# Spacing the first scores evenly over a turn, and putting the sums of exponentials last in ScalarE's slots

## The reference

```python
scores = einsum('bsnh,btnh->bnst', k, q) / sqrt(32)
scores = triu(scores) + -10000.0 * tril(ones, k=-1)
attn = softmax(scores, axis=2)
out = einsum('bnkq,bknh->bqnh', attn, v)
```

## Time and profile before

| what | us |
|---|---|
| median of 3 runs | 2469.89 (2462.67 to 2474.62) |
| the profiled execution, its own time | 2468.07 |
| its span in the trace | 2466.2 |
| TensorE busy | 2206.6 (89%) |
| ScalarE busy | 1648.3 (67%) |
| VectorE busy | 1519.0 (62%) |
| turns 2 to 15 | 1675.4, about 119.7 each |
| turn 16 | 113.0 |
| the experts | 425 |

### The profile page before, as it was taken

How to read it: one execution, slowest core, us unless ns; L and a number is a source line. 1 busy time by engine, 2 the same in 40 slices (tenths; PEclk the granted TensorE clock), 3 DMA queues, 4 the chain that set the end, 5 groups by cost and what they waited for, 6 DMA issues and landing times. The chain is left out here.

```text
span 2466.2 us, 48192 instructions
## 1 busy us (share of the span) xinstructions
PE 2206.6 (89%) x13674; PEld 1127.8 (46%) x13674; DVE 1519.0 (62%) x4937; ACT 1648.3 (67%) x4025; POOL 1125.4 (46%) x1622
## 2 busy tenths in 40 slices
PE   6679999999999999899989999999997776999997
PEld 3334444444444444344444444444443334666664
DVE  4545666666666575657666666666656554666664
ACT  5778686867676777677767767676765414666664
POOL 3223244444444443434444444444343534777775
PEclk9789999999999999999999999999998997999999
DMA  6022222222222222222222212121212017888885
GB/s 225 14 58 67 62 72 67 66 62 61 61 61 62 61 61 61 62 61 61 61 62 61 78 44 79 44 78 44 78 30 75 27 39 219 233 233 235 234 235 114
DMA packets 180907, 222.51 MB, mean 90 GB/s; under 512 B 37824, under 2 KB 119840, under 8 KB 180672
## 3 DMA queue, kind: packets, MB, share of 16 engines
q1 hardware_dynamic: 154048, 177.58, 24.4%
q0 software_dynamic: 26624, 42.12, 7.7%
HBM read 112.65 MB, written 56.46 MB: 69 GB/s over the span
## 5 line engine op out<-in xcount | busy, mean ns | idle before, releaser
L741 ACT ACTIVATE junk<-junk,nmax 128x512 f32<-128x512 f32 (+3 forms) x1024 | 571.6, 566 | 147.1 <-DVE nmax L1044 141.8
L1044 DVE CUSTOM_DVE_ANT_0 junk<-scores,maskrow 128x512 f32<-128x512 f32 (+3 forms) x1024 | 467.4, 487 | 192.9 <-PE scores L587 152.2
L731 ACT ACTIVATE probs<-scores_T 128x512 f32<-128x512 f32 x640 | 379.4, 600 | 69.1 <-PE scores_T L604 68.0
L1207 POOL TENSOR_SCALAR_AFFINE_SELECT probs<-probs 128x256 f32<-128x256 f32 x512 | 194.1, 415 | 383.4 <-ACT probs L731 383.0
L587 PE MATMUL scores<-stack_k,stack_q 96*128 96x512 f16 (+3 forms) x1024 | 252.0, 308 | 90.7 <-DVE nmax L1044 87.5
L1216 POOL DMA_INDIRECT slots_dram<-rec,idx x256 | 262.5, 1025 | 119.5 <-issue 106.9
L604 PE MATMUL scores_T<-stack_q,stack_k 97*128 97x512 f16 (+3 forms) x1024 | 252.8, 309 | 51.2 <-ACT probs L731 31.1
L1193 POOL TENSOR_TENSOR xres<-xres,bo 128x512 f32<-128x512 f32 x64 | 81.2, 1271 | 280.8 <-DMA xres<-in_x 280.8
L741 ACT ACTIVATION_READ_ACCUMULATOR junk<-junk,nmax 128x1 f32 x1024 | 207.3, 202 | 0.0
L211 PE MATMUL dense<-xT_hi,wqkv_hi 128*128 128x512 f16 x512 | 198.2, 387 | 1.5 <-DVE xT_lo L1014 1.5
L587 PEld LDWEIGHTS scores<-stack_k,stack_q 96*128 96x128 f16 x1024 | 97.1, 100 | 223.4 <-DVE nmax L1044 132.2
(11 more groups left out here) (234 smaller groups left out, 5560.3 us busy)
## 6 DMA issues: line engine op xcount, KB each, us to landing
stack_q<-split_q SPq DMA_DIRECT2D x384, 64.0 KB, 2.0
stack_k<-split_k SPq DMA_DIRECT2D x384, 64.0 KB, 2.4
out<-xres SPq DMA_DIRECT2D x67, 256.0 KB, 3.0
x2n<-in_x SPq DMA_DIRECT2D x64, 256.0 KB, 3.4
xres<-in_x SPq DMA_DIRECT2D x64, 256.0 KB, 2.7
x2n_dram<-x2n SPq DMA_DIRECT2D x16, 1024.0 KB, 4.4
ex_raw_wg<-in_W_gate SPq DMA_DIRECT2D x32, 512.0 KB
ex_raw_wu<-in_W_up SPq DMA_DIRECT2D x32, 512.0 KB
```

Source lines behind the costliest of these rows:

```text
L731: act.activation(to, at, ACT.Exp, scale=SCALE / (QS * QS)).then_inc(exp_done, 1)
L741: last = act.activation(x, x, ACT.Exp, scale=-1.0, bias=c["nmax"][:, hg % 2, m:m + 1], accum_out=c["sums"][:, hg % 2, m:m + 1])
L1044: last = dve.tensor_tensor_reduce(out=c["junk"][:, JUNK_AT[f], at:at + cols], in0=ps["scores"][f % 2][:, at:at + cols], in1=c["maskrow"][: ...
L1207: last = pool.affine_select(out=blk, in_=blk, compare_op=ALU.is_ge, fill=0.0, base=0, pattern=[[0, 2], [1, P]], channel_multiplier=-1)
```

## The change

Two edits. The first sets the slots of the first scores: one fill every two or three slots for group 1, and every three slots for groups 2, 3 and 0 over the rest of the turn. Since `MAX_SLOT`, `SUM_SLOT`, `NM_SLOT`, `SHIFT_SLOT` and `INV_SLOT` are derived from them, the maxima, the sums, the placing of the maxima and the inverses move along. The second edit moves `sums` and `shift_exps` behind everything else that ScalarE does in the same slot.

```diff
-S_AT = {1: range(1, 21, 2), 2: (23, 25, *range(31, 47, 2)), 3: (47, 49, 51, 53, *range(61, 73, 2)),
-        0: (83, 91, 94, 96, 99, 101, 104, 107, 110, 113)}
+S_AT = {1: (1, 4, 6, 9, 11, 14, 16, 19, 21, 24), 2: (27, 29, 32, 35, 38, 41, 44, 47, 50, 53),
+        3: (56, 59, 62, 65, 68, 71, 74, 77, 80, 83), 0: (86, 89, 92, 95, 98, 101, 104, 107, 110, 113)}
...
                     if attn and slot in READ_SLOT:
                         den_copy(i - 1, READ_SLOT[slot])
-                    if slot in SUM_SLOT:
-                        q, f = SUM_SLOT[slot]
-                        of = score_group(i, q, proj, attn)
-                        if of:
-                            sums(*of, f)
-                    if slot in SHIFT_SLOT:
-                        of = score_group(i, SHIFT_SLOT[slot], proj, attn)
-                        if of:
-                            shift_exps(*of)
                     if in_first(i) and slot in SPLIT_SLOT:
...
                     if attn and slot in AHI_SLOT:
                         att_hi(i - 1, AHI_SLOT[slot])
+                    if slot in SUM_SLOT:
+                        q, f = SUM_SLOT[slot]
+                        of = score_group(i, q, proj, attn)
+                        if of:
+                            sums(*of, f)
+                    if slot in SHIFT_SLOT:
+                        of = score_group(i, SHIFT_SLOT[slot], proj, attn)
+                        if of:
+                            shift_exps(*of)
```

## The result

| | before | after |
|---|---|---|
| median, us | 2468.66 (4 runs, 2462.67 to 2474.62) | 2557.03 (4 runs, 2554.61 to 2567.89) |
| ratio after to before | | 1.0372 [1.034, 1.0404] |
| span of the profiled execution | 2466.2 | 2552.6 |

The account below looks back on a forecast made before the run. TensorE, busy 2206.6 us, sets the pace. Terms 1.8 + 2.7 - 0.4 - 4.4 + 2.8 + 0.5 - 0.3 give 2.7 us a turn, 38 in 14; with turn 16's 5, 43 off 2468.07: 2426 median, range 2385 to 2485.

Parts of the forecast that it names:

- The waits for maxima: TensorE ahead of first scores, turns 3 to 14: fall from about 4.5 to below 1.5 us a turn.
- The new wait at slot 90: Group 3's first second score waits for placed maxima behind gate1's multiplication: 4.4 us a turn, bounds 2.6 to 5.3.
- the order alone: ScalarE's sums last in a slot: shorter waits at product with v and gate, 0.5 us a turn won.
- rival C: Slot 90's new wait is short, 2.6 us, if ScalarE's standstill goes with the order: 2385 us, chance 0.2.
- Group 1: 1.8 us a turn won, 0.4 lost: Fills up to slot 24: later fill 9 saves 1.8; placed maxima bring a new 0.4 wait.
- the forecast wait at slot 30: Group 1's second score waits for placed maxima after the later fill 9: 0.4 us.
- Group 3: 2.7 won: Fills from 56 to 83: x2T copies between spaced fills, high halves before sums, save 2.7 us a turn.
- Later waits: 2.8 regained: Behind slot 90 ScalarE and VectorE catch up while TensorE waits: 2.8 us a turn, bounds 0 and 3.5.
- The clock: 0.3 lost: TensorE's low-clock stretches: some go with removed waits, the new wait brings one; 0.3 us a turn lost.
- rival B: TensorE loses its clock every turn behind new waits, half the late waits stay: 2464 us, chance 0.19.
- Turn 16, forecast to win 5: Last fills with little dense work: spacing wins 7 us, placed maxima take some 2 back.
- Rival D: Standstill also catches group 3's sums; slot 90 wait 8.7 us, over 7 decides: 2523, milder 2492 less 5; chance 0.17.

Follow-up runs that it names:

- e2: Kernel before with only the new order on ScalarE (sums and shifts last in a slot), old slots of the first scores: 2427.76 us, ratio 0.9979 to before.
- e7: Changed kernel with each SyncE store issued ahead of the load of the tile before, last eight stack copies after: 2421.64 us, ratio 0.9968 to before.
- e11: Kernel before with SyncE's stores issued ahead of the residual loads: 2435.62 us, ratio 0.9878 to before.
- e12: Changed kernel with group 3's last fill at slot 82 instead of 83 and stores ahead of the loads: 2453.69 us, ratio 0.9942 to before.
- e14: Kernel before, old slots, with sums last in a slot and stores ahead of the loads: 2411.46 us, ratio 0.9779 to before.
- e18: Old slots with groups 0 and 3 spread (group 3's first four and last fills unmoved), sums last, stores ahead: 2428.09 us, ratio 0.9871 to before.
- e15: Changed kernel without GpSimd's scatters into the slot table (output not the reference's): 2466.99 us, 91 less than with scatters on the same chip.
- e16: Kernel before without GpSimd's scatters into the slot table: 2422.41 us, ratio 0.9833 to before.
- e17: Old slots with group 0 alone spread as in the change (86 to 113), sums last, stores ahead of the loads: 2391.79 us, ratio 0.9727 to before.
- e14_again: Repeat in a later session of old slots, sums last in a slot, stores ahead of the loads: 2410.89 us, ratio 0.979 to before.
- after_again: Changed kernel unaltered, run again on a chip without ScalarE standstills: 2480.78 us, ratio 1.0214 to before.
- e8: Kernel before with the new order, group 1 spread, group 2 begun at slot 27, the rest old: 2442.44 us, ratio 1.0052 to before.

## Why the prediction was wrong

**Right.** TensorE sets the pace, and only its waits could be won. The waits for maxima went. The new wait at slot 90 has the price, the place and the chain that were written down (4.55 for 4.4 us a turn, with 0.43 of the 4.55 for two fills that the forecast had not counted there); down waits less; the order alone is worth little. Where ScalarE does not stand still, slots 84 to 90 take 2.4 us more (9.02 against 6.63 in e2), which is the 2.6 of rival C.

**Group 1: 1.8 us a turn won, 0.4 lost.** Slots 0 to 24 got 0.9 longer, with one fill fewer, and 24 to 30 1.4, with one more. The step that failed: a wait of TensorE was taken as time to be had, without asking what TensorE would meet next. The sign was in the earlier trace rows: 0.79 us for the triangles in slot 24. I used it only to correct a time. Behind it was the late residual load, shown by e7: 59 us in the changed kernel, 28 in the kernel before (e11). SyncE's queue at the turn's end was named in front of the prediction as holding stores and residual loads, and was not followed to a landing. The load is not the whole answer: with the stores ahead in both, the new slots still take 0.5 us more in slots 0 to 30 (e12 against e14), of the size of the forecast wait at slot 30, which then appears. The 1.8 is won in no run.

**Group 3: 2.7 won.** Slots 60 to 74 were to be shorter and are 0.7 longer. The step that failed: "the x2T copies fall between fills three slots apart, and the high halves precede the sums". True within a slot, but the sums now precede the next slot's exponential, and TensorE waits for that. The waits for maxima in slots 60 to 74 went (2.1 us a turn before, none after) and 3.1 us for exponentials came. With the last fill and the loads out of play, e18 prices this at 36 us, 2.6 a turn, and e12 against e14 at 3.5 in slots 60 to 84. The term had the wrong sign.

**Later waits: 2.8 regained.** The waits of slots 90 to 108 did go: 2.5 us of idle a turn before, 0.5 after. Where the clock stayed at 1.00 these slots got 2.1 us shorter (15.93 in e15 against 18.02 in e16, one fill of 0.22 among it). On the chip of the result they got only 0.6 shorter, since they ran at a granted clock of 0.89: 17.96 us x 0.11 = 2.0 a turn. So this term was nearly right, and what is missing from it belongs to the clock. Its reason was in part luck: e17 shows that it needs no wait at slot 90. Group 0's spacing by itself makes slots 90 to 108 1.7 us shorter (16.31 against 18.01 in e14_again), and slots 84 to 108 1.3, with one fill more in these. I had put all of it down to engines catching up.

**The clock: 0.3 lost.** This is the mis-sized term. Busy time grew by 24.2 us in 14 turns, 1.7 a turn, where rival B had said 1.6; the slots that lost most are 90 to 108 behind the wait at slot 90, and 24 to 30 behind the wait for the triangles, at 0.89 and 0.82. The Trainium skill, TensorE: Matmul & The Clock Gate, section HAM oscillation, tells of a kernel in which TensorE waits for a DMA in every round of its loop and starts every round at the low clock. The trace agrees for the waits at slot 90 and slot 24, with 0.57 and 0.50 behind two of them. It is not so of every wait that comes in each turn: behind the 1.8 us at slot 90 in after_again the granted clock was 1.00 in slots 84 to 108. The e7 pair has the same in reverse: 28 of 58 us won were busy time.

**Sum.** Taken: 2.7 a turn won. Measured: 6.4 a turn lost. The difference of 9.1 is 3.7 in slots 0 to 30 (2.3 longer for 1.4 shorter), 3.6 in slots 60 to 84 (0.9 for 2.7 shorter) and 2.2 in slots 90 to 108 (0.6 shorter for 2.8), less the 1.0 that slots 30 to 60 gave (0.43 of it two fills fewer), and 0.6 in small ones; the clock is in these. Turn 16, forecast to win 5, lost 0.3: there too other waits took the place of those for maxima. Rival D named a slower end, at 2523 or 2487 (the range ended at 2485, though it was said to hold the second), but its mechanism (a wait at slot 90 over 7 us) is not what happened: that wait was 3.5 to 4.5 us in turns 3 to 14, and 7.6 only in turn 15. Rival B had the loss of clock, at the right price, and not the two waits that stood behind the removed ones. The rivals all varied the wait I had found. None said that another wait would stand behind a removed one, in two places at once.

**Still open.** What holds ScalarE while GpSimd prepares scatters, and why only on some chips. Whether odd slots alone cure the exponentials' wait. What made slots 30 to 54 longer in e8. Sums-last is worth 0.2% alone (e2) and about 1% with the stores ahead (e14 against e11), and the slots suggest why, though the first pair ran without a trace of the kernel before: against e16, e2 takes 1.1 us a turn less in slots 60 to 74 and 0.7 more in slots 0 to 30, where the late load waits; e14 against e11 takes 1.4 less in slots 60 to 74 and gives back only 0.1 in slots 0 to 30.

## What to carry to other kernels

Before a wait is booked as a gain, follow what the same engine needs within the next few microseconds back through every queue, DMA queues with their landings included: where two chains end near each other, removing one wins little until the other goes. And price a new wait with the clock that TensorE is granted behind it, not by its length alone: here four microseconds of waiting cost another two. An evenly spaced producer is not a smooth one; what counts is where its follow-up work (here the sums) falls in the order of the engine that the bottleneck waits for. And a DMA queue in which a store waits behind a load that waits for a store's landing runs at the pace of round trips: issue what is ready first.

## What the hardware showed that was not expected

ScalarE stands still, for nothing that the records name, until 0.7 to 1.4 us after the last of a row of GpSimd's indirect DMAs, and this depends on the chip: 59 us ahead of the tanh and about as much ahead of the copy of att in turns 2 to 15 on the chip of the result, none on the chips where the kernel before takes 2432 to 2434. Without the scatters the standstills are gone and both kernels are within 0.6% of their times there. The kernel before differs by 1.3% between the two kinds of chips; that the standstills are the reason is likely from this, and not shown by itself; what the change costs goes from 2.1% on a chip without them to 3.8% on one with them.

TensorE's clock was granted in full behind a 1.8 us wait that came in every turn, and in part only (0.89 over the next 18 slots) where the same wait was 3.5 to 4.5 us.
